# Graph attention layers on one core: the node stage in two passes over pairs of blocks, new x and the running total in pieces

## What is computed

```python
for l in range(3):
    f1 = relu(x[row] @ nb_W[l] + nb_b[l])
    f2 = relu(x[col] @ self_W[l] + self_b[l])
    h = relu(concatenate([f1, f2], axis=1) @ att1_W[l] + att1_b[l])
    log_alpha = (h @ att2_W[l] + att2_b[l])[:, 0]
    mask = clip(sigmoid(log_alpha) * (ZETA - GAMMA) + GAMMA, 0.0, 1.0)
    rowsum = segment_sum(mask, row, num_segments=n) + 1e-06
    d_inv_sqrt = clip(rowsum ** (-0.5), 0.0, 10.0)
    vals = mask * d_inv_sqrt[row] * d_inv_sqrt[col]
    x = segment_sum(vals[:, None] * x[col], row, num_segments=n)
    out = out + x
x = layernorm(x0 + out)
```

## Time and profile before

| what | us |
|---|---|
| median of 3 runs | 9865.02 (9862.49 to 9868.52) |
| the profiled execution, its own time | 9852.52 |
| its span | 9850.6 |

### The profile page before, as it was taken

One profiled execution on the slowest core, in us unless ns is written; L12 is line 12 of the kernel. 1 busy time (PEld: TensorE's weight loads), 2 busy tenths in 40 slices (PEclk: granted clock), 3 DMA queues, 4 the chain that ended last, 5 costly groups with the idle time before them and its releaser, 6 DMA issues.

```text
span 9850.6 us, 206958 instructions
## 1 busy us (share of the span) xinstructions
PE 6201.2 (63%) x44403; PEld 5462.9 (55%) x44722; DVE 7410.5 (75%) x29659; ACT 2922.9 (30%) x7919; POOL 6194.6 (63%) x6324
## 2 busy tenths in 40 slices
PE   3145555555569986555555549997555555556997
PEld 1135455455458875454554548886555545555886
DVE  8867777777768886777777768886777777776888
ACT  0021111111137772111111117774111111114776
POOL 0017777777755545777777765554777777775553
PEclk7565555555569996555555559998555555557998
DMA  0012222233254442222232254443222222326444
GB/s 21 0 42 71 71 71 72 71 71 72 71 94 119 118 113 67 71 72 71 71 72 71 71 65 125 118 119 82 72 71 71 71 71 71 72 71 100 118 118 99
DMA packets 921874, 778.05 MB, mean 79 GB/s; under 512 B 697300, under 2 KB 700660, under 8 KB 921460
## 3 DMA queue, kind: packets, MB, share of 16 engines
q0 software_dynamic: 199680, 368.45, 18.2%
q1 hardware_dynamic: 722164, 409.31, 15.2%
HBM read 620.19 MB, written 157.08 MB: 79 GB/s over the span
## 4 chain that ended last, share of the span: by engine, by line
PE 28%; POOL 25%; issue 19%; DVE 14%; ACT 8%; DMA 7%; ACTq 1%; DVEq 0%; POOLq 0%; SPq 0%
POOL k_hot L435 11%; PE bank L461 10%; POOL got L435 10%; PE bank L534 6%; PE bank L566 6%; DMA got<-qx_table,index 4%; POOL g_hot L435 4%; ACT p_all L671 3%; DVE acc L796 2%; DVE acc L797 2%; PE bank L571 2%; ACT onehot_t L686 2%; ACT p_all L682 2%; DMA k_hot<-qx_table,index 1%; PE bank L524 1%
## 5 line engine op out<-in xcount | busy, mean ns | idle before, releaser
L534 PE MATMUL bank<-p_all,onehot_t 128*128 x10032 | 2301.4, 424 | 1628.7 <-issue 1619.1
L534 PEld LDWEIGHTS bank<-p_all,onehot_t 128*128 128x128 f32 x10032 | 2186.7, 330 | 1679.7 <-issue 1679.7
L435 POOL DMA_INDIRECT got<-qx_table,index x2496 | 2391.5, 958 | 798.5 <-issue 758.6
L448 POOL DMA_INDIRECT got<-y_table,index x1248 | 1354.3, 1085 | 1163.7 <-ACT index L704 653.7
L653 ACT ACTIVATE small<-small 128x8 f32<-128x8 f32 x624 | 130.2, 209 | 5101.7 <-DVE small L920 5101.7
L461 PE MATMUL bank<-mask,onehots 128*128 128x3 bf16 x4992 | 676.4, 184 | 1265.8 <-DVE mask L931 1265.8
L435 POOL DMA_INDIRECT g_hot<-qx_table,index x1248 | 1199.4, 961 | 380.3 <-issue 377.6
L435 POOL DMA_INDIRECT k_hot<-qx_table,index x1248 | 1198.6, 960 | 380.3 <-issue 364.8
L461 PEld LDWEIGHTS bank<-mask,onehots 128*128 128x128 bf16 x4992 | 519.3, 104 | 1536.0 <-issue 1428.8
L967 DVE SCALAR_TENSOR_TENSOR p_all<-iota_b,col_hi,bank 128x104 f32<-128x104 bf16 x3768 | 952.1, 315 | 290.0 <-PE bank L566 289.9
L896 DVE TENSOR_SCALAR onehots<-iota_b,rows_now 128x128 bf16<-128x128 bf16 x5040 | 917.0, 289 | 22.5
(11 more groups left out here) (160 smaller groups left out, 9901.6 us busy)
## 6 DMA issues: line engine op xcount, KB each, us to landing
p_all<-col_rows SPq DMA_DIRECT2D x474, 256.0 KB, 3.7
kept_x<-got SPq DMA_DIRECT2D x312, 256.0 KB
k_x<-kept_x SPq DMA_DIRECT2D x312, 256.0 KB
got<-qx_table,index POOLq DMA_INDIRECT x2496
kept_x<-g_hot SPq DMA_DIRECT2D x156, 256.0 KB
p_all<-kept_x SPq DMA_DIRECT2D x156, 256.0 KB
g_hot<-qx_table,index POOLq DMA_INDIRECT x1248
k_hot<-qx_table,index POOLq DMA_INDIRECT x1248
```

Of the source, the lines that this page charges most:

```text
L435: pool.indirect_dma_start(got[j][:, k, :], None, qx_table, bass.IndirectOffsetOnAxis(ap=index[j][:, k:k + 1], axis=0)).then_inc(a_got[j], 16)
L448: pool.indirect_dma_start(got[j][:, k, 0:HID], None, y_table, bass.IndirectOffsetOnAxis(ap=index[j][:, k:k + 1], axis=0)).then_inc(g_got[j ...
L534: last = mm(bank_p[h][:, k, :], onehot_t[h][:, k, :], p_all[:, ds(ids[k], 1), :].rearrange("p o d -> p (o d)"), start=True, stop=True)
```

## The change

The node stage becomes two passes of 13 steps; a step has 8 blocks. Two blocks of 64 features lie side by side in the 128 rows of the array, with weights that are block diagonal (`w_cur[:, k, :]` and `a1_cur[:, k, :]`; the loads fill two copies of every weight and bias, and `w_all` and `a1_all` are cleared first). Pass k = 0 makes Q only, pass k = 1 makes P only.

- PE turns pairs of blocks straight from `x_cur`, in pass 0 alone, two steps ahead; the turned x stays in `acc` for pass 1. The product of step s+1 is issued before the second product of step s. Pass 0 is unrolled; pass 1 is a loop.
- POOL copies x of a step into the right half of `got[j]` (four buffers instead of `x_step`), DVE copies Q into the left half, and SP stores both with one transfer per step.
- POOL's gathers wait for the stores of pass 0 and for nothing of pass 1.
- DVE adds `x_cur` to `total` step by step in pass 1. The new `x_cur` is made in 13 pieces, each with its own signal `n_x`, and DVE no longer waits for it before the loop turns; PE turns the first two steps before the new weights are there.

```diff
-        x_step = ring("x_step", [PARTS, GRP, HID], F32)
-        q_step = ring("q_step", [PARTS, GRP, HID], F32)
+        f_t = [hidden[h][:, :, :].rearrange("p k d -> p (k d)") for h in range(2)]
+        w_cur = sb("w_cur", [PARTS, 2, PARTS], F32)
+        a1_cur = sb("a1_cur", [PARTS, 2, PARTS], F32)
```

On SP:

```diff
-                sp.dma_start(qx_rows[:, :, HID:2 * HID],
-                             x_cur[:, :, :]).then_inc(n_xst, 16)
-                        sp.wait_ge(n_q[h], l * NODE_STEPS + b + 1)
-                        sp.dma_start(qx_rows[:, ds((b * 2 + h) * GRP, GRP), 0:HID], q_step[h][:, :, :]).then_inc(n_qst[h], 16)
+                def store_step(s, b, j):
+                    sp.wait_ge(n_q, node_done(l, 0, s))
+                    sp.wait_ge(n_xs, l * NODE_STEPS + (s + 1))
+                    sp.dma_start(qx_rows[:, of_step(s), :], got[j][:, :, :]).then_inc(n_qst[j], 16)
```

On POOL:

```diff
-                        pool.tensor_copy(x_step[h][:, :, :],
-                                         x_cur[:, ds((b * 2 + h) * GRP, GRP), :]).then_inc(n_x[h], 1)
+                    pool.wait_ge(n_x, l * NODE_STEPS + (s + 1))
+                    pool.wait_ge(n_qst[j], stores(l, (b, j)) * 16)
+                    pool.tensor_copy(got[j][:, :, HID:2 * HID], x_cur[:, of_step(s), :]).then_inc(n_xs, 1)
+                for j in range(4):
+                    pool.wait_ge(n_qst[j], stores(l + 1, (0, j)) * 16)
```

On PE, the three kinds of work and their order in a step (`h` is the step's parity):

```diff
+                def turn_nodes(s, h):
+                    pe.wait_ge(n_x, l * NODE_STEPS + (s + 1))
+                    pe.wait_ge(n_xtc, l * NODE_STEPS + (s - 1))
+                    for i in range(GRP):
+                        last = turn(bank[h][:, i * PARTS:(i + 1) * PARTS],
+                                    x_cur[:, s * (2 * GRP) + 2 * i:s * (2 * GRP) + 2 * i + 2, :].rearrange("p b d -> p (b d)"), ident_f[:, :])
...
+                def node_step(k, s, h, ahead):
+                    if ahead > 1 and k == 0:
+                        turn_nodes(s + 2, h)
+                    if ahead > 0:
+                        first_product(k, s + 1, 1 - h)
+                    second_product(k, s, h)
+                turn_nodes(0, 0)
+                turn_nodes(1, 1)
                 pe.wait_ge(n_cur, l + 1)
+                first_product(0, 0, 0)
```

On ACT, which in a step does `hide(k, s)` and then, in pass 0, `keep_nodes(s + 2)`:

```diff
+                def keep_nodes(s, h):
+                    act.wait_ge(n_xt, l * NODE_STEPS + (s + 1))
+                    a.copy(acc[:, of_step(s), :].rearrange("p b d -> p (b d)"), bank[h][:, :]).then_inc(n_xtc, 1)
+                def hide(k, s, h):
+                    act.wait_ge(n_f, node_done(l, k, s))
+                    a.activation(f_t[h], bank[2 + h][:, :], ACT.Relu, bias=bias_cur[:, k:k + 1]).then_inc(n_fc, 1)
```

On DVE:

```diff
-            v.tensor_copy(x_cur[:, :, :], total[:, :, :])
+            for s in range(NODE_STEPS):
+                v.tensor_copy(x_cur[:, of_step(s), :], total[:, of_step(s), :]).then_inc(n_x, 1)
...
-                v.tensor_tensor(total[:, :, :], total[:, :, :], x_cur[:, :, :], ALU.add).then_inc(l_end, 1)
+                def give_columns(s, b, j):
+                    dve.wait_ge(n_pq, node_done(l, 0, s))
+                    dve.wait_ge(n_qst[j], stores(l, (b, j)) * 16)
+                    v.tensor_copy(got[j][:, :, 0:HID], bank[4 + j % 2][:, :].rearrange("p (b d) -> p b d", d=HID)).then_inc(n_q, 1)
+                def keep_rows(s, h):
+                    dve.wait_ge(n_pq, node_done(l, 1, s))
+                    v.tensor_tensor(p_all[:, of_step(s), :], bank[4 + h][:, :].rearrange("p (b d) -> p b d", d=HID),
+                                    b1_cur[:, :].unsqueeze(1).to_broadcast([PARTS, 2 * GRP, HID]), ALU.add).then_inc(n_q, 1)
+                    v.tensor_tensor(total[:, of_step(s), :], total[:, of_step(s), :], x_cur[:, of_step(s), :], ALU.add)
...
-                v.tensor_tensor(x_cur[:, :, :], acc[:, 0:NB, :], d_wide, ALU.mult).then_inc(l_end, 1)
-                dve.wait_ge(l_end, l * 3 + 3)
+                for s in range(NODE_STEPS):
+                    v.tensor_tensor(x_cur[:, of_step(s), :], acc[:, of_step(s), :], d_wide[:, of_step(s), :],
+                                    ALU.mult).then_inc(n_x, 1)
```

171 lines of the change are left out of this document (97 added, 74 removed).

## The result

| what | before, us | changed, us |
|---|---|---|
| median in the same comparison (6 runs each) | 9865.23 | 9790.89 |
| ratio, with 95% interval | | 0.9924 [0.9914, 0.9934] |
| the profiled execution, its own time | 9852.52 | 9792.93 |
| its span | 9850.6 | 9791.1 |

The change makes the kernel 74 us faster; 101 us were forecast. The time lies inside the range. The page's first part is almost that of before: the gain is not in busy time but in how early the gathers start.

A forecast was written before the change was run, and what follows sets the result against it. POOL's gathers were taken to bound the look stage, with the node stage a pure prologue. Terms: 2 x (8.5 + 26.0) + 33.7 - 1.9 = 100.8 us off, median 9865.0 to 9764 us, range 9740 to 9794.

The forecast's parts named there:

- Up to F: Layers 2 and 3, new x to PE's first product: 11.6 us instead of 20.2, 8.5 us less.
- the second rival: Node stage: PE takes 58.0 us, not 53, and POOL's copies wedge between DVE's pieces; about 9786 us; 15%.
- PE's work: Node stage from F: 53 us plus 4.4 for the low clock; row pass ends on DVE at F + 59.
- PE bounds both passes: Column and row passes: PE, at 2.3 and 1.8 us a step, stays the bound over all other engines.
- The first gather: Between the passes: POOL starts gathering at F + 39.6 instead of F + 72.3, 32.7 us earlier.
- The last rival: Gathers wait for pass 1 after all, or the passes stand in a row with POOL; 9813 us; 3%.
- What is late next: Look stage's fourth group: starts at F + 76.5 after one 6.7 us POOL stall; 26.0 us less per layer.
- Layer 1: Layer 1's node stage: 8 us less before F, 0.9 lost on x_cur pieces, 26.6 after; 33.7 us gained.
- The rule weighed: Row pass: each DVE add to total costs a gather beside it 0.1 us; thirteen cost POOL 1.4 us.
- The clock didn't stay low: Rival, node stage: TensorE's clock stays at 0.50, 53 us become 106; slower than before, 9907 us; 4%.
- DVE did catch up: Rival denying this, look stage: DVE or PE never catch up, a group takes 10 us, not 8.1; 9809; 9%.
- The first rival: Look stage: POOL's start alone counts, no stall at the fourth group; 32.7 instead of 26.0 us per layer, 9744; 8%.

The follow-up runs named there:

- e3_wait_turn: Changed kernel with DVE's wait for the last piece of new x put back inside the layer loop, ahead of its turn; 9767.57 us, ratio 0.9927 to before.
- f4_best: f3_adds_in_columns with POOL's copies of x also waiting for all 13 pieces of the new x; 9752.42 us, ratio 0.9889 to before.
- f1_no_lookahead: Changed kernel with PE making the next step's first product behind this step's second product; 9854.65 us, ratio 0.9993 to before.
- e1_index_early: Changed kernel with ACT's three first index copies moved from behind the row pass to ahead of the column pass; 9737.56 us, ratio 0.9896 to before.
- a0_after: The changed kernel unaltered, run again on the chip of three experiments; 9761.58 us, ratio 0.992 to before.
- e2_wait_pass1: Changed kernel with POOL's gathers made to wait for the last step of the row pass as well; 9769.59 us, ratio 0.9929 to before.
- f2_early_spread: e1_index_early with acc also cleared in pieces between the look stage's groups instead of all at once ahead; 9767.59 us, ratio 0.9903 to before.
- f3_adds_in_columns: f2_early_spread with DVE's adds to total moved from the row pass into the column pass; 9757.32 us, ratio 0.9893 to before.

## Why the prediction held, and where it did not

Point by point, by its own numbers. F is PE's first product.

1. *Up to F.* Forecast 11.6 us after the start of new x, found 10.1. Two terms were off and partly cancelled: the turn's 3.0 us, which I had kept, is gone altogether (e3_wait_turn brings back 3.01), and the pieces take 9.56 us instead of 7.9, since POOL's copies wedge themselves in, as the second rival said (f4_best has 7.92 without them).
2. *PE's work.* PE's last product of the row pass ended at 6755.90 + 2.17, F + 53.5, forecast F + 57.4 (53 and 4.4 for the low clock). The low clock lasted for 4.6 us of work instead of 8.8 and so cost 2.3 us; the work itself comes out at 51.2. The row pass ended on DVE at 6758.95 + 0.74, F + 55.1, forecast F + 59. Steps were 2.19 and 1.75 us, forecast 2.3 and 1.8. My choice of 53 over the 58 of the printed durations was near, and that the new order leaves PE no wait in the row pass is in the rows; f1_no_lookahead shows what such waits cost.
3. *PE bounds both passes.* Right for the row pass: no idle before PE's rows, 0.42 to 0.49 us idle before each of DVE's steps.
4. *The first gather.* Forecast F + 39.6, found 6757.71, F + 53.2. **This is the step that failed.** I read POOL's order and the stores and took the indices of the first three groups as ready at once, as the kernel before has them. They are made by ACT behind the whole node stage. In the kernel before that cost nothing: they were made at 6818.56 (L639), and the last Q was ready for its store only at 6820.84; now a second pass stands between the last store and that place. The last rival named the outcome (the gathers wait for pass 1 after all), had it at 3%, and set against it only the order of POOL's instructions, which doesn't speak about ACT's. It also had the start too late, at F + 63: the indices follow the last Relu of the row pass, not DVE's last piece and a store behind it. e1_index_early shows the cause: with those three copies of 0.38 us in all elsewhere, the first gather is at F + 35.0, even 4.6 us before my figure, as the column pass was shorter than I had it.
5. *What is late next.* Forecast the 25th gather at F + 76.5 with a stall of 6.7 us, found F + 84.2 without one. The chain on which I built it was right in each link: from the row pass' end to the first L997 are 6773.22 - 6759.69 = 13.5 us, as said, and L725 follows 3.5 us behind it. It only didn't decide, since the gathers themselves were later. They also took 31.0 us for 24 where I had 30.2, by one of 1.45 us beside DVE's L999 among others. In e1_index_early, where the chain does decide, the 25th gather is at F + 72.7. Its own links are 54.5 to the end of the row pass (6727.32 + 0.68), 13.7 to L997 and 4.5 to the gather, where the forecast had 59, 13.5 and 4.0.
6. *Layer 1.* The 25th gather came 727.3 - 703.2 = 24.1 us earlier, forecast 33.7 less 1.0 for the clearing. The first product gained 624.00 - 619.77 = 4.2 us, where 8 less 0.9 and 1.0 had been forecast. The 8 us came: from DVE's weight copies to the first product were 624.00 - 613.92 = 10.1 us and are 619.77 - 617.80 = 2.0. The two deductions were too small. DVE comes to the copy that makes x_cur 1.4 us later, and its 13 pieces take 6.09 us where one instruction took 3.62, so 2.5 us are lost and not 0.9. The first two rows are of the kernel before, the others of the changed one:

```profile
593.00 3.62 DVE L840 COPY x_cur<-total 128x6656 f32<-128x6656 f32 x1
...
613.92 0.22 DVE L874 COPY w_cur<-w_all 64x128 f32 x1 [0.24 <-DVE spots_of L862]
```

```profile
594.40 6.09 DVE L907 COPY x_cur<-total 128x512 f32<-128x512 f32 x13
...
617.80 0.29 DVE L941 COPY w_cur<-w_all 128x256 f32 x1 [0.24 <-DVE spots_of L929]
```

   The rest is point 4.
7. *Elsewhere.* New x of layer 1 starts 1.4 us later (forecast 1.0), the tail is 0.6 longer (0.9).

The sum: at the 25th gather layers 2 and 3 gained 29.3 and 28.4 us, forecast 34.5 each; with layer 1 that is 81.8 instead of 101.7. So the failed step costs more than it seems to: by e1_index_early 9.7 to 11.2 us per layer, of which points 1 and 2 gave some 5 back by luck. The range held because its width was there for PE's term, not for the one that failed. That the time, 9790.9, lies near the second rival's 9786 is chance too: of that rival only the wedged copies came true, not the longer PE steps.

The medians differ by 74 us, the two profiled executions by only 59.6. Between their 25th gathers' 81.8 and this lie the rest of the look stages (12.4 us longer in the three layers together), the sum stages (9.2) and the tail (0.6); what makes the sum stages longer I can't assign. One plain property of the profiled runs goes with the first of these: the gathers in that of the changed kernel took 947 ns at the median, in that of before 944 (min/median/max of the largest group, before, then changed):

```profile
L435 POOL DMA_INDIRECT got<-qx_table,index x2496: 940/944/1465, 696.9 to 8906.8; - x192
```

```profile
L454 POOL DMA_INDIRECT got<-qx_table,index x2496: 940/947/1613, 672.4 to 8844.1; - x192
```

If every one of 6240 gathers is 3 ns longer and POOL is what the stage waits for, that is an estimated 19 us. It doesn't seem to belong to the kernel: the changed kernel has 947 here and 944 in a0_after. On the chips of normal pace, the profiled executions with 944 lie within 3.3 us of their own kernel's median in five of six cases (a0_after, e2_wait_pass1, e3_wait_turn, f1_no_lookahead, f4_best), and that of the kernel before lies 12.7 us below its median. Of those with 947, e1_index_early, f2_early_spread and f3_adds_in_columns lie 11 to 19 us above theirs, and the changed kernel 2.0. Why an execution has one or the other no run shows.

**The rule weighed.** I had a price of 0.1 us for a gather beside a DVE instruction with two SBUF inputs, from one row. e1_index_early shows 0.5 (1.43 to 1.46 against 0.95), and f3_adds_in_columns shows that it is those adds, since without them every gather of the pass is 0.94 to 0.97. My row was misread: L915 had started 0.46 us before that gather and had only 0.2 us left.

```profile
1386.97 0.69 DVE L915 SCALAR_TENSOR_TENSOR hidden<-hidden,a_cur 128x512 f32<-128x512 f32 x1
```

The gather of e1_index_early at 6720.92 met an add with 0.6 us left and took 0.5 longer; so did that at 6773.99 in the changed kernel beside L999. A piece of the new x and a POOL copy lengthen each other alike: 1.10 and 1.07 us against 0.68 and 0.62. The Trainium skill, "SBUF — State Buffer", section "SBUF: two separate sides", has it that a DVE operation with two SBUF inputs and a GpSimd operation that reads the SBUF lock each other out for a whole instruction. The runs agree with that. It hardly moved the forecast, because in the changed kernel the gathers come when the adds are all but over.

**The rivals.** The clock didn't stay low. L997 kept its pace of 8.0 us without data waits (6773.22, then 6781.23), so DVE did catch up. The first rival's sign, no idle before the 25th gather, is there: POOL's start alone decided, only at F + 53.2 and not at the F + 39.6 on which that rival's 9744 rests. With the start early (e1_index_early) the stall is back, 3.5 us, and POOL's start doesn't decide.

## What to carry to other kernels

When a change lets an engine start earlier, list every producer of what that engine needs, and for each one look at what stands ahead of it in its own in-order queue, above all the tiny ones: here three copies of 0.38 us in all held POOL back by 10 to 11 us a layer. Fewer and wider instructions pay only if their order leaves the engine no wait: with the next step's first product behind this step's second the whole rewrite came to next to nothing (0.9993). Work moved from one place to another can be paid for there: the clearing in pieces made some 50 gathers per layer longer. And where one forecast stall is absent from the new trace, ask what came late ahead of it, before calling the forecast of it wrong.

## What the hardware showed that I had not expected

- The wait for the last piece ahead of the loop's branch cost DVE 3.01 us of idle time; without that wait, with the same branch, none (6694.44 + 9.56 to 6703.93). The branch itself is hidden.
- A DVE add of two SBUF tensors (0.68 us) cost a POOL gather that started with it 0.5 us (0.95 to 1.43 and more, e1_index_early), and a piece of the new x, which reads two SBUF tensors as well, cost a POOL copy beside it 0.45 (0.62 to 1.07, changed kernel). A DVE copy of 0.22 us from SBUF to SBUF cost a gather 0.16 (0.95 to 1.11, f2_early_spread).
- The granted clock rose from 0.50 to 1.00 (from 1.2 to 2.4 GHz) 4.6 us after the first product. In the kernel before it rose at about 6758.7 (0.50 up to 6758, a mean of 0.83 from 6758 to 6760), 6.8 us after the first product and 8.6 us after PE had begun to turn at 6750.07. In the changed kernel PE had turned two steps at 6695.19, and the clock was at 1.00 until about 6698.9 (a mean of 0.74 from 6698 to 6700); whether that is the reason was not tested.
- The gathers of one execution can be 3 ns longer at the median than those of another of the same kernel, on another chip (944 in a0_after, 947 in the changed kernel's own profile), an estimated 19 us of 9790 over all gathers.
